# Quantized feed-forward of a two-layer transformer block on one core: input rounding moved to GpSimd a group ahead, a third of the gated products split over ScalarE and GpSimd, the clip of the down input split between ScalarE and VectorE

## The reference

```python
def _act_fake_quant(x, clip_factor):
    scale = jax.nn.sigmoid(clip_factor) * jnp.max(jnp.abs(x)) / QMAX      # QMAX = 127
    return jnp.clip(_ste_round(x / scale), -QMAX - 1.0, QMAX) * scale
def _weight_fake_quant(w):
    scale = jnp.max(jnp.abs(w), axis=1, keepdims=True) / QMAX
    return jnp.clip(_ste_round(w / scale), -QMAX - 1.0, QMAX) * scale

xq = _act_fake_quant(x, clip_x[0])
gate = jnp.einsum('bsh,ih->bsi', xq, _weight_fake_quant(w_gate))
up = jnp.einsum('bsh,ih->bsi', xq, _weight_fake_quant(w_up))
h = _act_fake_quant(jax.nn.silu(gate) * up, clip_down[0])
return jnp.einsum('bsi,hi->bsh', h, _weight_fake_quant(w_down))

x = x + jnp.tanh(g_ffn[1]) * _L1_ffn_ref(_layernorm(x, axis=-1), ...)
```

## Time and profile before

| | us |
|---|---|
| median of 3 runs | 2420.72 |
| the profiled execution, its own time | 2418.37 |
| its span, first to last instruction | 2416.6 |
| PE busy | 2070.6 (86%) |
| VectorE (DVE) busy | 1707.5 (71%) |
| ScalarE (ACT) busy | 1236.6 (51%) |
| GpSimd (POOL) busy | 664.6 (28%) |

### The profile page before, as it was taken

One profiled execution on the slowest core, in us unless ns is written; L12 is line 12 of the kernel. 1 busy time (PEld: TensorE's weight loads), 2 busy tenths in 40 slices (PEclk: granted clock), 3 DMA queues, 4 the chain that ended last, 5 costly groups with the idle time before them and its releaser, 6 DMA issues.

```text
span 2416.6 us, 39292 instructions
## 1 busy us (share of the span) xinstructions
PE 2070.6 (86%) x14938; PEld 1260.6 (52%) x14938; DVE 1707.5 (71%) x2821; ACT 1236.6 (51%) x2936; POOL 664.6 (28%) x537
## 2 busy tenths in 40 slices
PE   5688788888876569999999999999999978899566
PEld 2343555555543334444566666666666646667223
DVE  3557676675878789976576767777777766676677
ACT  1365786858654256545333333333333476676346
POOL 0334876768656344000000000000000033344003
PEclk6788899999987679999999999999999999999776
DMA  4221000000000057454755544455445440000002
GB/s 136 73 72 52 1 1 1 1 2 3 2 1 1 1 197 283 197 211 182 213 158 155 158 149 157 152 156 149 159 149 159 127 136 1 1 1 1 0 1 70
DMA packets 125100, 221.79 MB, mean 92 GB/s; under 512 B 16828, under 2 KB 61745, under 8 KB 124785
## 3 DMA queue, kind: packets, MB, share of 16 engines
q1 hardware_dynamic: 109810, 168.32, 23.0%
q10 hardware_dynamic: 15103, 50.97, 5.3%
HBM read 152.50 MB, written 65.67 MB: 90 GB/s over the span
## 4 chain that ended last, share of the span: by engine, by line
PE 52%; DVE 29%; ACT 11%; issue 4%; DMA 2%; POOL 1%; SPq 1%; DVEq 0%; ACTq 0%
PE ps L446 48%; DVE arena L960 13%; DVE arena L969 7%; ACT arena L1890 4%; DVE arena L963 4%; PE ps L454 4%; ACT arena L1639 3%; DVE arena L966 2%; DVE arena L976 2%; ACT arena L1898 1%; ACT arena L1741 1%; SPq L2072 1%; ACT arena L1742 1%; ACT arena L1643 0%; DMA arena<-share_scratch 0%
## 5 line engine op out<-in xcount | busy, mean ns | idle before, releaser
L446 PE MATMUL ps<-arena 128*128 128x512 f16 (+10 forms) x13708 | 1918.8, 299 | 164.0 <-ACT arena L1639 37.5
L446 PEld LDWEIGHTS ps<-arena 128*128 128x128 f16 (+6 forms) x13708 | 1107.1, 102 | 895.9 <-issue 151.1
L960 DVE TENSOR_TENSOR arena<-arena 128x512 f32<-128x512 f32 (+7 forms) x958 | 720.6, 781 | 163.4 <-ACT arena L1845 111.6
L1639 ACT ACTIVATE arena<-ps,arena 128x512 f32<-128x512 f32 (+2 forms) x480 | 323.6, 686 | 248.1 <-PE ps L446 159.5
L960 DVE TENSOR_TENSOR arena<-ps,arena 128x512 f16<-128x512 f32 (+10 forms) x427 | 227.7, 554 | 252.5 <-ACT arena L1643 64.2
L1845 ACT CAST arena<-arena 128x512 f16<-128x512 f32 x256 | 158.2, 618 | 458.0 <-DVE arena L960 456.0
L1945 POOL TENSOR_TENSOR arena<-arena 128x4 f32<-128x4 f32 (+3 forms) x50 | 85.1, 1703 | 1102.8 <-DVE arena L963 1102.0
L2002 POOL TENSOR_TENSOR arena<-arena 128x512 f16<-128x512 f32 (+1 forms) x288 | 346.0, 1222 | 105.3 <-ACT arena L1639 103.9
L454 PE MATMUL ps<-arena 128*128 128x128 f32 (+2 forms) x1230 | 216.3, 310 | 176.1 <-DVE arena L963 94.6
L966 DVE SCALAR_TENSOR_TENSOR arena<-ps,arena 128x512 f32<-128x512 f32 (+4 forms) x317 | 220.6, 698 | 185.7 <-PE ps L446 138.3
L1639 ACT ACTIVATE arena<-ps 128x512 f16<-128x512 f32 (+1 forms) x512 | 273.4, 606 | 71.5 <-PE ps L446 66.9
(11 more groups left out here) (76 smaller groups left out, 485.4 us busy)
## 6 DMA issues: line engine op xcount, KB each, us to landing
arena<-share_scratch SPq DMA_DIRECT2D x512, 128.0 KB, 3.0
wide_scratch<-arena ACTq DMA_DIRECT2D x96, 512.0 KB, 2.6
arena<-wide_scratch SPq DMA_DIRECT2D x96, 512.0 KB, 4.5
mq_scratch<-arena SPq DMA_DIRECT2D x16, 308.0 KB
vw_scratch<-arena SPq DMA_DIRECT2D x32, 154.0 KB
arena<-mq_scratch SPq DMA_DIRECT2D x16, 308.0 KB, 5.3
arena<-vw_scratch SPq DMA_DIRECT2D x8, 576.0 KB, 6.1
arena<-in_x SPq DMA_DIRECT2D x4, 1024.0 KB, 11.9
```

The lines of the kernel that those rows point to most:

```text
L446: return e.matmul(o, l, r, start=start, stop=stop, skip_group_check=True)
L960: return e.tensor_tensor(o, a, b, op)
L1639: return e.activation(o, i, f, bias=bias, scale=scale)
```

## The change

- GpSimd rounds the groups 1 to 7, two instructions each: the multiplication with the addition of MAGIC, then both clips around MAGIC. It is a group ahead of its use: group 1 at once, group g + 2 behind its first product of group g. VectorE rounds only group 0. Behind group 1 GpSimd clears the 64 rows of H that no chunk fills.
- Of each group the units c = 1 and c = 4 (not the very last c = 4) are POOLED. ScalarE makes the Silu into FSp and also up x scale into UPp, two buffers each, and GpSimd multiplies the two into H. VectorE only reads the peak, two units later. The up bank comes free with ScalarE's copy. ScalarE and PE do `whole(g + 1)` behind c = 3 and c = 2.
- Down input: VectorE does H x 1/scale + MAGIC on the five chunks, two groups ahead, ScalarE on the chunk of 64 rows. ScalarE then does Relu(H + 128 - MAGIC) over all six chunks into bfloat16 (the lower clip), and VectorE, in place in bfloat16, the minimum with 255 and the subtraction of 128.
- The Sigmoid stands behind ATTEND. The statistics of the last group's first three tiles stand ahead of the residual step of tile 30.
- The last down group is evicted, added and stored in two halves.

```diff
+    FSp, UPp = [[Y_.take([512]) for _ in range(2)] for _ in range(2)]
+    ATTEND.insert(ATTEND.index(("gather", NT - 1)), ("early_stats", 7))
+    POOLED = [n for n in range(46) if n % 6 in (1, 4)]
+    TURN = {n: [m in POOLED for m in range(n)].count(n in POOLED) for n in range(48)}
...
         def whole(g):
-            W.wait_ge("xq", g + 1)
+            W.wait_ge("xq" if g else "sg", g or 2)
...
+            empty[n % 3], empty[3 + n % 3] = [("fsl", n + 1)], [("fu" if n in POOLED else "fh", TURN[n] + 1)]
...
+                if g == 7 and t == 1:
+                    m.then_inc(S["dn"], 1)
...
-        def whole(g):
-            W.after(W.own(ts(XH[g], XH[g], s[:, 9:10], -128.0, ALU.mult, ALU.max)))
-            ts(XH[g], XH[g], 127.0, MAGIC, ALU.min, ALU.add).then_inc(S["xq"], 1)
+        W.after(W.own(ts(XH[0], XH[0], s[:, 9:10], -128.0, ALU.mult, ALU.max)))
+        ts(XH[0], XH[0], 127.0, MAGIC, ALU.min, ALU.add).then_inc(S["sg"], 1)
...
+            if n not in POOLED:
+                W.wait_ge("fgu", 2 * n + 2)
+                W.wait_ge("fsl", n + 1)
+                stt(H[0:r_, c, 512 * g:512 * g + 512], bank(3 + n % 3)[0:r_], sgx[0:r_, 6 + c:7 + c], FSb[TURN[n] % 2][0:r_],
+                    ALU.mult, ALU.mult).then_inc(S["fh"], 1)
+                a = peak(n)
+                if n >= 2 and n - 2 in POOLED:
+                    peak(n - 2)
...
+        def scaled(g):
+            v = H[:, 0:5, 512 * g:512 * g + 512]
+            ts(v, v, s[:, 11:12], MAGIC, ALU.mult, ALU.add).then_inc(S["ha"], 1)
+
+        def clipped(g):
+            W.wait_ge("hlo", g + 1)
+            ts(HQ[g % 2], HQ[g % 2], 255.0, 128.0, ALU.min, ALU.subtract).then_inc(S["hq"], 1)
+
+        scaled(0)
...
         for g in range(8):
+            clipped(g)
+            if g < 6:
+                scaled(g + 2)
             if g:
                 finish(g - 1)
...
+            W.wait_ge("fhp" if n in POOLED else "fh", i - 1)
+            fn((FSp if n in POOLED else FSb)[i % 2][0:r_], bank(n % 3)[0:r_], ACT.Silu,
+               scale=sgx[0:r_, c:c + 1]).then_inc(S["fsl"], 1)
+            if n in POOLED:
+                W.wait_ge("fgu", 2 * n + 2)
+                e.activation(UPp[i % 2], bank(3 + n % 3), ACT.Copy, scale=sgx[:, 6 + c:7 + c]).then_inc(S["fu"], 1)
+            if c == 3 and g < 7:
                 whole(g + 1)
...
+        rest = [scaled_rest(0), scaled_rest(1)]
         for g in range(8):
+            W.wait_ge("ha", g + 1)
+            W.after(rest[g])
             W.wait_ge("dn", g - 1)
+            fn(HQ[g % 2], H[:, :, 512 * g:512 * g + 512], ACT.Relu, bias=nml).then_inc(S["hlo"], 1)
+            if g < 6:
+                rest.append(scaled_rest(g + 2))
...
+        def whole(g):
+            W.after(W.own(e.tensor_scalar(XH[g], XH[g], s[:, 9:10], MAGIC, ALU.mult, ALU.add)))
+            e.tensor_scalar(XH[g], XH[g], MAGIC + 127.0, MAGIC - 128.0, ALU.min, ALU.max).then_inc(S["xq"], 1)
...
+        whole(1)
+        W.wait_ge("xq", 1)
+        e.memset(H[64:128, 5, :], 0.0).then_inc(S["const"], 1)
+        W.wait_ge("const", 15)
+        for i, n in enumerate(POOLED):
+            g, c = divmod(n, 6)
+            W.wait_ge("fsl", n + 1)
+            W.wait_ge("fu", i + 1)
+            e.tensor_tensor(H[:, c, 512 * g:512 * g + 512], FSp[i % 2], UPp[i % 2], ALU.mult).then_inc(S["fhp"], 1)
+            if c == 1 and g < 6:
+                whole(g + 2)
```

More of the change, by code:

```diff
@@ L972, in cp, with stats @@
             return e.tensor_copy(o, i)
-        def stats(g, done="var", folded=False):
-            for i in range(4 * g, 4 * g + 4):
+        def stats(g, done="var", folded=False, first=0):
+            for i in range(4 * g + first, 4 * g + 4):
                 m = e.bn_stats(st6[:, i % 4, :], xs[:, i, :])
             W.after(W.own(m))
-            for i in range(4 * g, 4 * g + 4):
+            for i in range(4 * g + first, 4 * g + 4):
                 m = e.bn_aggr(mv[:, i, :], st6[:, i % 4, :])
@@ L1524, in vector @@
                 normed(mxh, g)
+            elif x[0] == "early_stats":
+                W.wait_ge("x2", 4 * x[1] + 3)
+                for i in range(4 * x[1], 4 * x[1] + 3):
+                    m = e.bn_stats(st6[:, i % 4, :], xs[:, i, :])
+                W.after(W.own(m))
+                for i in range(4 * x[1], 4 * x[1] + 3):
+                    e.bn_aggr(mv[:, i, :], st6[:, i % 4, :])
             elif x[0] == "last_stats":
                 W.wait_ge("x2", 4 * x[1] + 4)
-                stats(x[1], "fvar")
+                stats(x[1], "fvar", first=3 if x[1] == 7 else 0)
             elif x[0] == "last_norm":
@@ L1584, in vector @@
             r_ = 128 if c < 5 else 64
[L1585 to L1592, removed]
+            if n not in POOLED:
[6 more added lines that the diff above has]
+                    peak(n - 2)
         W.after(a)
         whole_max(1, hm, 10, 3)
-        W.after(W.own(tt(s[:, 12:13], s[:, 10:11], gat[:, 7:8], ALU.mult)))
+        W.own(tt(s[:, 12:13], s[:, 10:11], gat[:, 7:8], ALU.mult))
+        def scaled(g):
[5 more added lines that the diff above has]
+        scaled(0)
+        W.last()
         for k in range(2):
@@ L1599, in vector @@
             ts(dg, ident, s[:, 14 + k:15 + k], None, ALU.mult).then_inc(S["dgk"], 1)
+        scaled(1)
         W.wait_ge("sdm", 2)
         sd = W.own(cp(SD, bank(7)[:, 0:256]))
[L1603 to L1608, removed]
         def finish(g):
@@ L1864, in side @@
         def side(x):
-            if x == ("begin", 0):
-                W.wait_ge("w2", 128)
-                fn(s[:, 2:4], s[:, 0:2], ACT.Sigmoid).then_inc(S["gates"], 1)
-            elif x[0] == "flip":
+            if x[0] == "flip":
                 src, k, c0 = x[1:]
@@ L1905, in scalar @@
                 side(x[1])
+        W.wait_ge("w2", 128)
+        fn(s[:, 2:4], s[:, 0:2], ACT.Sigmoid).then_inc(S["gates"], 1)
         def whole(g):
-            W.wait_ge("const", 13)
             for k in range(2):
@@ L2197, in sync @@
                 W.wait_ge("fo", g + 1)
+                load("out", ov[:, 4 * g:4 * g + 4, :], xs[:, 4 * g:4 * g + 4, :])
             else:
-                W.wait_ge("y2", 9)
-            load("out", ov[:, 4 * g:4 * g + 4, :], xs[:, 4 * g:4 * g + 4, :])
-        W.wait_ge("out", 128)
+                for i in (28, 30):
+                    W.wait_ge("y2", i // 2 - 6)
+                    load("out", ov[:, i:i + 2, :], xs[:, i:i + 2, :])
+        W.wait_ge("out", 144)
     block = ctx.enter_context(nc.Block())
```

74 lines of the change are left out of this document (38 added, 36 removed).

## The result

The changed kernel takes 2364.49 us (median of 4 runs, 2362.39 to 2368.34), the kernel before beside it 2421.44 (4 runs, 2419.73 to 2424.29): a ratio of 0.9765, 95% interval 0.9749 to 0.9782. Forecast were 2367, and 2357 to 2392. The profiled execution took 2362.39 us with a span of 2360.6; the one before had 2416.6, so 56.0 us less.

The account below looks back on a forecast made before the run. No engine was full in the gate and up loop; it ran at VectorE's pace, with serial waits for its rounding. Terms -2.7 - 1.3 + 1.0 - 44.4 - 6.0 - 0.7 = -54.1 gave 2367 us, range 2357 to 2392.

Parts of the forecast that it names:

- (1): Attention loop: moving the Sigmoid to the hand-over removes two table loads of 1.28 us; gain 2.7 us (0 to 2.8).
- (2): Before the last residual step: three of the last four bn_stats and their aggregates move ahead; gain 1.3 us (1.0 to 1.4).
- (3): Hand-over: GpSimd rounds group 1 while VectorE rounds group 0, each blocking the other; loss 1.0 us (0 to 2.3).
- (4): Gate and up loop of 48 units: VectorE stays the bound, 66 us against 110.4; gain 44.4 us (40 to 47).
- (5): From the last peak to the first down product: PE starts at 9.0 us instead of 10.9; gain 1.9 us.
- (6): Eight down groups: 4.85 us a group, 38.8 in all; gain 6.0 us with the 1.9 of (5) in it.
- (7): End of the kernel: output in halves shortens the last DMA; gain 0.7 us (0 to 0.8).
- P: Time of a tensor_scalar of 1024 columns on GpSimd, used in its rounding; taken as 1.5 us (1.2 to 2.34).
- B: Loop: GpSimd becomes the bound from P = 2.3 on; P = 3.2 gives 2376 us, P = 4 2387; chance 0.11.
- C: Loop: GpSimd makes the kernel slower than before from P = 6.4 us on, 2443 at P = 8; chance 0.02.
- rival A: Loop: PE's clock stays at 1.2 GHz, gain 10 us, time 2401; low half the time, about 2384; chance 0.13.
- rival D: Gains outside the loop swallowed by another wait and by VectorE and GpSimd blocking each other; 8.7 us go, 2376; chance 0.06.

Follow-up runs that it names:

- sig_back: The changed kernel with the Sigmoid put back into the attention loop; 2363.96 us, ratio 0.9764 to the kernel before.
- no_early: The changed kernel with the last group's statistics read all at once again after its last chunk; 2370.47 us in one run.
- ahead_only: The kernel before with one edit: VectorE rounds the loop's input a group ahead, nothing on GpSimd, nothing split; 2394.35 us, ratio 0.9891.
- scale_last: The changed kernel with VectorE's down-stage order clip, evict, scale instead of clip, scale, evict; 2364.77 us, ratio 0.9760.
- swap_late: The changed kernel with the order clip, evict, scale in the down stage from group 2 on only; 2362.52 us, ratio 0.9768.

## Why the prediction was right

| step | predicted | measured |
|---|---|---|
| (1) Sigmoid | -2.7 | -2.4 |
| (2) early statistics | -1.3 | -1.2 |
| (3) rounding of group 1 | +1.0 | +0.7 |
| (4) loop | -44.4 | -48.4 |
| (5) up to the first down product | -1.9 | -2.2 |
| (6) down groups | -4.1 | -2.45 |
| (7) halves | -0.7 | -0.3 |
| sum | -54.1 | -56.3 |

The spans differ by 56.0; the remaining 0.3 is the unchanged part. Two errors of opposite sign offset each other in part: 4.0 us too little in the loop, 1.65 too much in the down groups. That the sum is off by only 2 us is to that extent luck. Two of the prediction's sums are slightly off: 55.2 less 49.3 is 5.9 and not 6.0, and all good ends together make 2358 and not 2357; neither changes the outcome.

*(1), (2)* held, by sig_back's and no_early's traces. ScalarE's first later load is at 2223.68, in idle time.

*(3)* The mechanism held: the second rounding instruction of VectorE takes 1.5 instead of 0.7 us. The size P was wrong: a tensor_scalar of 1024 columns takes GpSimd 1.04 to 1.12 us undisturbed, below my lower bound of 1.2 and under half of its two-input add (2.35). Clearing 4096 columns took 3.51, where I had 4. That refutes rivals B and C, which need P over 2.3; no row of the kernel before could have excluded them.

*(4)* The bound was right, VectorE with 4 x 1.38 + 2 x 0.59 = 6.7 us a group, and so was the clock. What failed is the term "0.4 a group for waits between four engines with nearly equal load": there is none, 6.69 being VectorE's sum. That is 3.2 us. The 6.0 us before the first product held (5.97), the first group, at the low clock, cost some 1.8 instead of 2.4 (an estimate: 62.2 us to the end of the last peak, less 5.97 and VectorE's sum of 54.4). Against rival A stands the clock of 1.00 in the middle of the loop; and ahead_only keeps 2.4 GHz almost throughout with PE busy 78% of the time (23.49 of 30 us in 2270 to 2300).

*(5)* PE starts 8.5 us after the maximum, where I had 9.0. The clip of 3072 bfloat16 columns takes 0.94, I had 0.95. By the Trainium skill (VectorE: DVE Perf Modes, Mode 4×_2P), four elements a cycle, it would be 0.8 plus start, an estimate: the trace agrees.

*(6)* The 5.8 us of the groups with scaling are 5.82 (the first of them 6.13). The mean of 4.85 a group was too low: from the first product to the last eviction the eight groups take 40.44 us, 5.06 each. The step that failed is the time of PE's products in it, "5.3 at the low clock, 2.65 at the high one". The clock of the changed kernel in this stage (windows of its trace):

```profile
2336.00:2338.00 2.00, 2.00 (x12) 1.09 (x11) 2.00 (x1) 0.61 (x1) 1.21 (x1) 0.68 0.00 0
...
2338.00:2350.00 12.00, 11.10 (x46) 4.96 (x45) 9.87 (x7) 5.71 (x2) 7.15 (x3) 0.50 0.28 94
```

The 24 products of a group take 3.56 us at the high clock and about 6.0 at the low one (group 5: 2340.97 to 2347.0, all at 0.50; the 4.92 of group 4 are mixed, since the clock falls within them). I halved the time of the low clock, but products of 256 columns don't double their speed (0.148 us each at the high clock; those of 512 columns 0.214). So the ring of product, Relu and clip (two quantized tiles, each filled anew when its products are done) ends the stage: the two groups without scaling cost 2.50 and 4.93 us, in them ScalarE waits 4.10 us for PE, and the last clip waits for GpSimd (1.93 instead of 0.94). Of rival D the half on VectorE and GpSimd was true, and in the sum already. By these two traces step (6) gained 2.45 us instead of 4.1. The size of that error is not sure: (5) and (6) together are 4.65 here, but with the old down stage at 54.95 or 57.03 and the new one at 50.18 to 51.21 they are anything from 3.7 to 6.9, and 6.0 was forecast. No run isolates the clock's part.

*(7)* The last DMA ends 3.07 us after the last addition, before 3.4. The prediction took half of that time to go with the size. But from issue to landing a store of 256 KB takes 2.9 us and one of 512 KB 3.0 (medians of this trace), so nearly all of it is independent of the size. The higher share of the DMA engines in the last window, 0.72 instead of 0.49, is that of more than the last half: 241 GB/s over 3.1 us are some 750 KB.

## What to carry to other kernels

- An operation that a loop needs once in a group is worth more for where it stands than for its length: 1.47 us of rounding cost 4 us a group as long as PE, ScalarE and again VectorE waited for it in turn, and its removal a group ahead gave 30 of the 48 us.
- In this loop, where a group or two of buffers decouple the engines, the period was the largest engine's sum of work (9.66, 8.27, 6.69), and an addition for interaction was wrong. Between engines in a ring, as in the down stage, the sum failed: what scale_last and swap_late took from the steady groups came back in the groups around them.
- Two changes that each save less than the spread of a run are judged by stage lengths in the trace, with the stages ahead of them taken out; and stages that the change leaves alone, in the other traces, tell how much such a length wanders (here 1 us, in the old down stage 2).

## What the runs showed of the hardware

- GpSimd's tensor_scalar (multiply and add, f32, 128 x 1024) takes 1.04 to 1.12 us, its tensor_tensor of the same size 2.35; two inputs cost twice as much and more.
- VectorE and GpSimd hold each other up in both directions: GpSimd's addition 2.35 to 3.00 or 3.32 us (swap_late), its tensor_scalar 1.12 to 1.42, VectorE's rounding 0.7 to 1.5, and its bfloat16 clip 0.94 to 3.00 when the addition had begun just before. Evictions, with a source in PSUM, kept 1.20 to 1.23 us, also beside GpSimd's addition (1.23 at 2347.07 in the changed kernel, within GpSimd's 2345.85 to 2351.17).
- PE's clock stayed at 2.4 GHz for tens of microseconds with idle times of 0.2 to 1.6 us between products (ahead_only, 2287 to 2331: 1.00); behind idle times of 5 us, as at each hand-over, it was 1.2 GHz. In the down stage it fell just before 2337 behind waits of no more than 2.27 us, and came back at about 2350 with PE idle for only 0.9 of the 12 us between 2338 and 2350; why it fell there and not in the loop no run here tells.
- 24 products of 256 columns (bfloat16, each with its own weights) took 3.56 us at 2.4 GHz and about 6.0 at 1.2, 0.148 and 0.25 us each: less than a factor of two between the clocks. Those of 512 columns took 0.214 us each at 2.4 GHz and 0.43 at 1.2 (their weight loads start 0.43 us apart at the beginning of the loop, from 2250.68 on in the kernel before).
